# Two PSUM banks for the spread of B, two instead of three for the other matmul results

## The reference

```
xn = layernorm(x)
# block 1: selective state space model, 256 channels, 16 states
xr = rmsnorm(xn) * norm_w ;  xi, z = split(xr @ W_in)
xc = silu(causal_conv(xi, 4 taps) + conv_b)
dt, B, C = split(xc @ W_x)                   # 64, 16, 16
dt = softplus(dt @ W_dt + b_dt)
h[t] = exp(dt * A) * h[t-1] + (dt * xc) * B  # one recurrence per channel and state
y = (sum over states of h * C + D_skip * xc) * silu(z)
s = xn + y @ W_out
# block 2: mixture of 8 experts, the best 2 per token
scores = normalised top 2 of softmax(xn @ Wg)
g = silu(sum over experts e of scores[e] * (relu(xn @ W1[e] + b1[e]) @ W2[e] + b2[e]))
out = x + s * g
```

## Time and profile before

| what | value |
|---|---|
| median of 3 runs | 411.31 us (409.33 to 412.11) |
| the profiled execution | 411.05 us |
| its span, first to last instruction | 409.2 us |
| matmul busy, weight loads busy | 365.3 us, 195.7 us |
| VectorE, ScalarE, GpSimd busy | 310.3, 214.2, 228.0 us |
| mean granted TensorE clock | 0.979 of full |

### The profile page before, as it was taken

The page is one execution under the profiler, slowest core; times in us unless marked ns, Lnnn a source line. Parts: engine busy times, 40 slices in busy tenths (PEclk is TensorE's granted clock), DMA queues, the critical chain, the costliest instruction groups (busy, mean ns, idle before and its releaser), DMA issues.

```text
span 409.2 us, 4166 instructions
## 1 busy us (share of the span) xinstructions
PE 365.3 (89%) x1287; PEld 195.7 (48%) x1287; DVE 310.3 (76%) x367; ACT 214.2 (52%) x402; POOL 228.0 (56%) x197
## 2 busy tenths in 40 slices
PE   0949999687799999896999999899799999999995
PEld 0323454255355644353555654355355564455554
DVE  3788966479968978598677868878868759976835
ACT  1267444873455444974463643986265535446630
POOL 3052285258365744478575744468574547766940
PEclk9988999998999999999899999999899999999999
DMA  7661011120020120110020203030020204100000
GB/s 214 204 256 55 2 36 67 16 91 1 1 103 34 70 74 30 67 40 0 2 103 19 85 0 104 0 106 2 0 103 2 103 1 110 45 0 0 2 26 26
DMA packets 9794, 22.48 MB, mean 55 GB/s; under 512 B 1399, under 2 KB 6894, under 8 KB 7726
## 3 DMA queue, kind: packets, MB, share of 16 engines
q1 hardware_dynamic: 9478, 21.71, 15.6%
q10 hardware_dynamic: 296, 0.53, 0.5%
HBM read 21.05 MB, written 1.18 MB: 54 GB/s over the span
## 4 chain that ended last, share of the span: by engine, by line
PE 69%; DVE 15%; ACT 7%; issue 4%; POOL 2%; DMA 1%; DVEq 0%; POOLq 0%; ACTq 0%
PE py L801 21%; PE px L878 11%; PE px L872 10%; PE pB L783 10%; PE px L837 6%; DVE hs L700 3%; DVE pdbu L691 2%; POOL hc L332 2%; PE px L884 2%; PE px L844 1%; PE px L850 1%; PE py L792 1%; PE px L826 1%; DMA x_sb<-in_L_attn_x 1%; DVE gs L651 1%
## 5 line engine op out<-in xcount | busy, mean ns | idle before, releaser
L332 POOL TENSOR_TENSOR hc<-hs,Ct 128x512 f32<-128x512 f32 x126 | 159.7, 1291 | 74.6 <-DVE hs L700 74.6
L700 DVE TENSOR_TENSOR_SCAN hs<-dec,pdbu 128x1024 f32<-128x1024 f32 x64 | 146.2, 2284 | 4.9 <-DVE pdbu L691 0.4
L801 PE MATMUL py<-hc,ident 128*128 128x512 f32 x256 | 123.4, 605 | 0.0
L691 DVE TENSOR_TENSOR pdbu<-u,pB 128x1024 f32<-128x1024 f32 x64 | 78.6, 1228 | 56.9 <-PE pB L783 54.6
L420 ACT ACTIVATE dec<-dt,negA 128x512 f32<-128x512 f32 x128 | 87.8, 721 | 9.1 <-DVE hs L700 8.8
L801 PEld LDWEIGHTS py<-hc,ident 128*128 128x128 f32 x256 | 48.1, 192 | 57.1 <-issue 53.4
L878 PEld LDWEIGHTS px<-w,hT 128*128 128x128 f32 x512 | 63.5, 196 | 19.5 <-issue 12.7
L783 PE MATMUL pB<-dtp,sel 128*128 128x512 f32 x128 | 67.1, 606 | 4.7 <-DVE pdbu L691 4.7
L872 PE MATMUL px<-xnT,w 128*128 128x512 f32 x128 | 66.7, 615 | 5.0 <-ACT xnT L459 4.4
L514 ACT ACTIVATE hT<-px,cols 128x512 f32<-128x512 f32 x64 | 43.7, 687 | 51.4 <-PE px L872 43.4
L384 POOL TENSOR_TENSOR acc<-acc,ysc 128x512 f32<-128x512 f32 x29 | 37.6, 1295 | 57.3 <-ACT ysc L503 49.4
(11 more groups left out here) (102 smaller groups left out, 249.4 us busy)
## 6 DMA issues: line engine op xcount, KB each, us to landing
Ct<-c_rows SPq DMA_DIRECT2D x16, 1024.0 KB, 4.7
w<-in_L_ffn_W SPq DMA_DIRECT2D x1, 1024.0 KB
out<-xn SPq DMA_DIRECT2D x4, 256.0 KB, 4.3
x_sb<-in_L_attn_x SPq DMA_DIRECT2D x1, 768.0 KB, 5.6
u<-in_L_attn_conv_w ACTq DMA_DIRECT2D x1, 512.0 KB, 4.6
x_sb<-in_L_attn_x SPq DMA_DIRECT2D x1, 256.0 KB, 5.2
win<-in_L_attn_W_in SPq DMA_DIRECT2D x1, 256.0 KB, 4.1
wout<-in_L_attn_W_out SPq DMA_DIRECT2D x1, 128.0 KB
```

What stands on the lines that cost most here:

```text
L332: eng.tensor_tensor(hc[:, n % HC_RING, b, :], hs[:, n % HS_RING, b, :], Ct[:, g % C_RING, s % PIECE, :], ALU.mult).then_inc(hc_last if n = ...
L691: dve.tensor_tensor(pdbu[:, :, :], u[:, k % 2], pB[:, :, :].to_broadcast([P, DB, CH]), ALU.mult)\
L700: dve.tensor_tensor_scan(hs[:, n % HS_RING].rearrange("p b t -> p (b t)"), dec[:, n % DEC_RING].rearrange("p b t -> p (b t)"), pdbu[:, :, ...
L801: last = pe.matmul(py[:, b, :], ident[:, :], hc[:, n % HC_RING, b, :], start=False, stop=s == STATES - 1)
```

## The change

pB gets two banks, and unit n uses bank n modulo 2. TensorE issues the spreads of units 0 and 1 before the slots, and then in slot 2n + 1 that of unit n + 2 instead of n + 1; it waits for n - 1 products instead of n. AUX goes from 3 to 2, so that the fill of job j waits until job j - 2 has been emptied. The tables of jobs stay as they are.

```diff
-AUX = 3
+AUX = 2
...
-        pB = banks("pB", 1)
+        pB = banks("pB", 2)
...
-                dve.tensor_tensor(pdbu[:, :, :], u[:, k % 2], pB[:, :, :].to_broadcast([P, DB, CH]), ALU.mult)\
+                dve.tensor_tensor(pdbu[:, :, :], u[:, k % 2], pB[:, n % 2:n % 2 + 1, :].to_broadcast([P, DB, CH]), ALU.mult)\
                     .then_inc(dbu_done, 1)
...
-                if n > 0:
-                    pe.wait_ge(dbu_done, n)
-                pe.matmul(pB[:, 0, :], sel[:, s, :], dtp[:, k % 2, :], start=True, stop=True).then_inc(B_spread, 1)
+                if n > 1:
+                    pe.wait_ge(dbu_done, n - 1)
+                pe.matmul(pB[:, n % 2, :], sel[:, s, :], dtp[:, k % 2, :], start=True, stop=True).then_inc(B_spread, 1)
...
             spread_B(0)
+            spread_B(1)
             for n in range(END_SLOT + 1):
-                if n % 2 == 1 and n // 2 + 1 < UNITS:
-                    spread_B(n // 2 + 1)
+                if n % 2 == 1 and n // 2 + 2 < UNITS:
+                    spread_B(n // 2 + 2)
```

## The result

The changed kernel takes 423.88 us (median of 4 runs, 422.36 to 424.15) against 410.51 us before: ratio 1.0316, 95% interval 1.0268 to 1.0363. It is slower by 3.2%; the forecast was 422.6 us. Its profiled execution took 422.36 us, 11.3 us more than the profiled one of before (411.05). It is the fastest of the four; by the medians the change costs 13.4 us.

A forecast was written before the change was run, and what follows sets the result against it. TensorE, working its list in order, was taken as the bound, not VectorE's waits. Terms 10.4 + 2.2 + 0.5 - 1.5 = 11.6 us over 411.05 gave 422.6; own range 416 to 425, 8 in 10 for 415 to 429.

The forecast's parts named there:

- Rival A: VectorE is the bound and its waits for B are the price, so faster: 409.8 or 403.5 us; chance 0.05.
- The spread: Earlier spreads save 0.9 us at 352 us and 0.6 before the D_skip matmuls at 137.85; gain 1.5 us.
- the list holds as many spreads as before: Between the end of one gs wait and the next, TensorE's list has no fewer or more spreads.
- The start: z0 of chunk 0 waits for m1a's bank, and tr comes at 48.9 for 47.72: plus 1.2 us.
- dt, plus 2.9: dt of chunk 1 waits for m2b's bank: 2.9 us late, plus 1.2 for the clock, so 4.1.
- y2 and the gate: Chunk 0: y2 waits for gl's bank, its drain delays the gate's exponential, and VectorE begins on that 8.7 us late.
- the last clock loss: TensorE stands 4.4 us from 111.4 before the spread in chunk 0; half-level clock afterwards: plus 1.7, 10.4 in all.
- Middle chunks: m1b waits for m1a's bank, making gs 0.9 us late; y6 and m0b wait 0.1 each: plus 1.1 per chunk.
- Last chunk: m6a waits for y5's drain: plus 0.5 us.
- The part without the clock: Ring terms with no clock loss: 5.8 us for the three places of chunk 0, 2.2 middle chunks, 0.5 last chunk.
- The clock's part: Half-level clock of TensorE costs 1.2 us at dt, 1.7 at y2 and 1.7 before the spread of unit 13.
- Rival D: Some twenty fills with thin slack turn to waits, or short waits bring the half-level clock: 428.6 us; chance 0.10.

The follow-up runs named there:

- e1: The kernel before with only AUX changed from 3 to 2, the spread left single and one unit ahead: 423.1 us, ratio 1.0286.
- e9: e10 with the kernel before's spread (one bank, one unit ahead, its filling before unit 12), ring of two: 411.17 us, ratio 0.9991.
- e10: e8 with matmuls of constants cut to 3 before each gs and 5 before the spread of unit 13: 407.62 us, ratio 0.9914.
- e5: e1 with 24 matmuls of constants into the free bank before the long stands of TensorE: 416.44 us, ratio 1.0114.
- e7: The kernel before with 4 matmuls of constants before each gs of the middle chunks: 407.81 us, ratio 0.99.
- e8: The changed kernel with job tables fitted to a ring of two and matmuls of constants in four stands: 410.75 us, ratio 0.9972.
- e3: The changed kernel with gl filled after y2 instead of before m3b in chunk 0: 417.06 us, ratio 1.0145.
- e11: e9 with AUX = 3, a ring of three: 408.28 us, ratio 0.9908.
- e6: The changed kernel with 4 matmuls of constants before each gs of the middle chunks: 419.31 us, ratio 1.0181.

## Why the prediction was right, step by step

**What bounds the kernel.** Right: TensorE's list does, and VectorE's 54.6 us were not on the path. e1 against the changed kernel and e9 against e10 show it. Rival A falls: with 47% of weight loads TensorE was full wherever nothing stopped it. The Trainium skill (Perfetto Trace Analysis, Identifying the Most-Contended Engine) spoke for that rival; beside weight loads it names the share of peak arithmetic as a measure, which wasn't worked out here.

**The spread, 1.5 us of gain.** Right in two places, and one was overlooked. At 352 us the changed kernel gained 1.3 us on the kernel before (the lag of its jobs goes from 12.8 to 11.5 us between m1b and y0), forecast 0.9; at the D_skip matmuls of chunk 1 0.8, forecast 0.6. Overlooked: the list of the last chunk has one spread less (the lag goes from 11.5 to 10.7 us before y5), because the extra one at the start is covered by z0's wait. The step that said "the list holds as many spreads as before" holds for the middle chunks alone. In all about 2.9 us, and e9 against e10 measures 3.5: the term was too small by about half.

**The start, plus 1.2.** Mis-sized. The wait for m1a's bank came as worked out (z0 at 36.84), but 3.3 us at half level began with it, which I hadn't counted after so short a stand: z0 took 2.08 us and the spread 1.67. tr came 2.5 us late.

**dt, plus 2.9 on top of the start's 1.2.** The wait is right to 0.1 us relative to the start: its releaser is the drain of m2b. For the clock I took 1.2; dt ran wholly at half level, 1.8. So the chain was 6.2 us late instead of 4.1.

**y2 and the gate.** The mechanism is right: gl's drain, y2's fill at half level (3.73), its scalings, then the exponential. I forecast VectorE's start on it 8.7 us late; it was 106.98 - 96.10 = 10.9, that is the 2.1 from above and 0.1. The release of the spread was then 10.0 late, 0.9 less than its start: the small operations of the gate took 10.1 us instead of 11.0. The difference is in two that ran beside an instruction of GpSimd and ended 0.03 to 0.05 us after it. The CAST of L650 took 0.65 us before and 0.33 after (its end 101.37 and 111.34, GpSimd's 101.34 and 111.31), the product of L640 0.87 and 0.27 (97.40 and 107.68, GpSimd's 97.35 and 107.63). And the clock did *not* fall after the 3.34 us at that spread, for which I had 1.7. Terms of 10.4, measured 10.0: the start and dt were taken 2.1 us too small, the gate and the last clock loss 2.6 too large. That the sum fits is luck.

**Middle chunks, 1.1 each.** gs is later by 0.9 in each, as forecast, with the rest from y6 and m0b; chunk 1 adds 1.4 us in all (the waits at y6 and m0b, 0.1 each in the forecast, come to 0.2 to 0.3), chunk 2 2.3, of which about 1 is the longer stretch at half level (6.7 against 3.3 us). That gs stood as before, 3.63 for 3.65 us, is the clearest point against rival A.

**Last chunk, 0.5.** m6a waited 0.37 us and was late by 0.5.

**The sum.** Forecast 11.6, measured 11.3 in the profiled executions and 13.4 by the medians. The part without the clock was sized well as a whole (8.5 against the 8.6 of e5 and e7). The spread's gain was sized at 1.5 and is about 3. The clock's part was placed wrongly and sized too small: the forecast has 4.6 us of it (1.2 at dt, 1.7 at y2, 1.7 before the spread of unit 13). The ring alone has 3.5, which are e1's 12.1 over the kernel before less the 8.6, and the changed kernel has some 2.6 more behind its second gs. By this estimate 8.6 + 3.5 + 2.6 - 2.9 = 11.8. So too little gain and too little loss nearly cancelled, which is luck; what bounds the kernel, and where it would wait, was not.

Rival D, with waits spread thinly over twenty fills, didn't occur: from gs to y5 of chunk 1 the changed kernel stays behind by the same 10.3 us. The Trainium skill (TensorE: Matmul & The Clock Gate, A second HAM failure mode: psum-queue depth-cycling) describes a kernel that cycles through PSUM banks and whose clock swings by short and frequent idling. Here the clock fell with single stands, 1.69 us the shortest in the changed kernel, and not with m1b's 0.91 us, which was followed by 1.00 in both chunks, nor with the 3.34 us before the spread of unit 13.

## What to carry to other kernels

In these runs a bank taken from a ring cost time where the drain of the job N places before (N banks are left) came later than the fill: list these fills, give each its wait, and follow what the drained engine does next, since a late fill may stand in front of the very operation that the chain needs (y2's drain before the gate's exponential). A large total of waits on one engine by itself says nothing of the gain in removing them; 41 us less of them bought 3.5 here. And before the worth of a reordering is read from the total, look at the granted clock behind each stand of TensorE, or fill the stands with matmuls of constants, which alone gave 1% on the unchanged kernel. They must end before the stand does: e8 had three too many and e10 shows what these cost.

## What was not expected of the hardware

Whether the clock fell was not a matter of the stand's length alone. After stands of 3.6 to 3.7 us at gs it was at 0.50 in the changed kernel and in the kernel before, and at 1.00 in e3; it fell with z0's stand of 1.69 us, and not after 3.34 us before the spread of unit 13. After 1.30 us before the same spread near 94 us it fell in e9 and e10 and not in e11. The half level lasted 3.3 us in one chunk's gs and 6.7 us in the next, in one execution. So the same edit can be worth 1 us or 5, as e3 and e6 showed, by what it does to places that it doesn't touch. What sets this was not tried.
